# A graph layer in split fp32 matmuls: the first eight pieces of adj in two contiguous halves, with x, residual and statistics steps moved

## What is computed

```python
def _layernorm(x, axis=-1, eps=1e-05):
    m = jnp.mean(x, axis=axis, keepdims=True)
    v = jnp.var(x, axis=axis, keepdims=True)
    return (x - m) / jnp.sqrt(v + eps)

h = jnp.maximum(_layernorm(x, axis=-1), 0.0)           # x: (8192, 128) fp32
x = x + ((1.0 - 0.1) * (adj @ h) + 0.1 * L0_gnn_h)     # adj: (8192, 8192) fp32
```

## Time and profile before

| | |
|---|---|
| median of 3 runs | 717.7 us (717.62 to 717.85) |
| the profiled execution, its own time | 718.35 us |
| its span | 716.6 us |
| TensorE busy | 707.0 us (99%) |
| VectorE busy | 625.0 us (87%) |
| ScalarE busy | 521.3 us (73%) |
| read from HBM / written | 281.02 MB / 4.19 MB |
| mean over the span | 398 GB/s |
| granted TensorE clock | 1.00 |

### The profile page before, as it was taken

One profiled execution on the slowest core, in us unless ns is written; L12 is line 12 of the kernel. 1 busy time (PEld: TensorE's weight loads), 2 busy tenths in 40 slices (PEclk: granted clock), 3 DMA queues, 4 the chain that ended last, 5 costly groups with the idle time before them and its releaser, 6 DMA issues.

```text
span 716.6 us, 7886 instructions
## 1 busy us (share of the span) xinstructions
PE 707.0 (99%) x3076; PEld 575.3 (80%) x3076; DVE 625.0 (87%) x462; ACT 521.3 (73%) x342; POOL 27.6 (4%) x17
## 2 busy tenths in 40 slices
PE   7999999999999999999999999999999999999998
PEld 2777888888888888888888888888888888888886
DVE  3879998998999989998888888888888889888985
ACT  3878877869688796877767676676767767676773
POOL 1001102001020100200000000000000000000000
DMA  8999999999999999999999999999999999999991
GB/s 291 411 418 420 403 419 419 415 422 414 421 411 422 416 415 402 420 421 412 383 398 409 387 395 378 403 397 388 413 387 406 423 418 413 420 415 425 420 422 75
DMA packets 46117, 285.73 MB, mean 399 GB/s; under 512 B 5120, under 2 KB 5632, under 8 KB 14592
## 3 DMA queue, kind: packets, MB, share of 16 engines
q1 hardware_dynamic: 46080, 285.23, 98.2%
HBM read 281.02 MB, written 4.19 MB: 398 GB/s over the span
## 4 chain that ended last, share of the span: by engine, by line
PE 88%; DMA 4%; DVE 3%; issue 2%; ACT 1%; SPq 1%; POOL 0%; DVEq 0%; ACTq 0%
PE acc L428 16%; PE acc L429 16%; PE acc L433 16%; PE acc L417 13%; PE acc L412 13%; PE acc L406 13%; DMA raw<-wide_dram 4%; DVE a_lo L316 2%; SPq L190 1%; ACT a_hi L270 1%; POOL rstd L232 0%; ACT h_full L239 0%; DVE stats L282 0%; SPq L179 0%; DVE h_lo L308 0%
## 5 line engine op out<-in xcount | busy, mean ns | idle before, releaser
L316 DVE TENSOR_TENSOR a_lo<-raw,a_hi 128x2048 fp32r<-128x2048 f32 (+1 forms) x262 | 581.3, 2224 | 65.3 <-ACT a_hi L270 64.8
L270 ACT ACTIVATE a_hi<-raw 128x2048 fp32r<-128x2048 f32 (+1 forms) x262 | 487.7, 1865 | 175.3 <-PE acc L433 90.4
L428 PE MATMUL acc<-a_hi,h_hi 128*128 128x512 f32 x512 | 199.2, 389 | 0.0
L429 PE MATMUL acc<-a_hi,h_lo 128*128 128x512 f32 x512 | 199.2, 389 | 0.0
L406 PE MATMUL acc<-a_hi,h_hi 128*128 128x512 f32 x504 | 135.9, 390 | 3.0 <-ACT a_hi L270 3.0
L417 PE MATMUL acc<-a_lo,h_hi 128*128 128x512 f32 x504 | 135.8, 391 | 1.2 <-DVE a_lo L316 0.8
L433 PE MATMUL acc<-a_lo,h_hi 128*128 128x512 f32 x512 | 136.8, 389 | 0.0
L412 PE MATMUL acc<-a_hi,h_lo 128*128 128x512 f32 x504 | 134.8, 389 | 0.0
L406 PEld LDWEIGHTS acc<-a_hi,h_hi 128*128 128x128 f32 x504 | 94.1, 188 | 25.2 <-issue 2.9
L417 PEld LDWEIGHTS acc<-a_lo,h_hi 128*128 128x128 f32 x504 | 93.9, 188 | 23.8 <-DVE a_lo L316 4.6
L429 PEld LDWEIGHTS acc<-a_hi,h_lo 128*128 128x128 f32 x512 | 96.1, 188 | 20.0
(11 more groups left out here) (15 smaller groups left out, 26.9 us busy)
## 6 DMA issues: line engine op xcount, KB each, us to landing
raw<-tall_dram SPq DMA_DIRECT2D x128, 1024.0 KB, 8.7
raw<-wide_dram SPq DMA_DIRECT2D x118, 1024.0 KB, 9.8
raw<-wide_dram SPq DMA_DIRECT2D x16, 512.0 KB, 12.6
res_sb<-res_dram SPq DMA_DIRECT2D x16, 512.0 KB, 5.6
x_sb<-x_dram SPq DMA_DIRECT2D x15, 256.0 KB, 10.2
out_dram<-finished SPq DMA_DIRECT2D x15, 256.0 KB, 9.1
raw<-wide_dram SPq DMA_DIRECT2D x8, 256.0 KB, 6.4
out_dram<-finished SPq DMA_DIRECT2D x2, 128.0 KB, 1.8
```

Of the source, the lines that this page charges most:

```text
L270: nc.scalar.activation(a_hi[:, q % SPLIT_SLOTS, cols], raw[:, q % RAW_SLOTS, cols], ACT.Copy).then_inc(hi_ready, 1)
L316: nc.vector.tensor_tensor(a_lo[:, q % SPLIT_SLOTS, cols], raw[:, q % RAW_SLOTS, cols], a_hi[:, q % SPLIT_SLOTS, cols].bitcast(fp32), ALU.s ...
L428: nc.tensor.matmul(bank, h_hi[:, k, :], a_hi[:, slot, cols], start=(k == 0), stop=False)
L429: nc.tensor.matmul(bank, h_lo[:, k, :], a_hi[:, slot, cols], start=False, stop=False)
```

## The change

- Pieces 0 to 7 come in two parts of 128 x 1024 each, and the host lays each part out as one block (`early_dram`); so far pieces 0 and 1 came in four parts and 2 to 9 in two, cut out of the whole piece's layout. Pieces 8 and 9 now come whole.
- x unit 1 (blocks 4 to 7) is loaded before piece 4 instead of before piece 2; unit 2 before piece 6 instead of before piece 4.
- Statistics and aggregation of blocks 4 to 7 stand behind `a_lo` of piece 3 instead of before `h_lo` of unit 0; their shift behind piece 4, the scaling behind pieces 5 and 6, `h_lo` behind piece 7. For blocks 8 to 11 statistics start at piece 7 (was 5), the shift stands at 12 (was 10), scaling at 13 and 14 (was 12 and 13), `h_lo` at 15 (was 14).
- Residual load n stands behind piece 44 + 10n (was 12 + 12n), sum n behind 51 + 10n (was 20 + 12n), for n < 8.
- The warm-up is 15 matmuls of 256 columns (was 12 of 512).

```diff
-PARTS = {0: 4, 1: 4}
-PARTS.update({_q: 2 for _q in range(2, 10)})
+EARLY = 8
+PARTS = {_q: 2 for _q in range(EARLY)}
+PART = PIECE // 2
...
-    _d = 5 if _g == 3 else 2 * _a - 12 if _single else 2 * _a - 19
+    _d = 7 if _g == 3 else 2 * _a - 12 if _single else 2 * _a - 19
...
-        _s = _end + 3 + 2 * (_u - _a // UNIT)
+        _s = _end + (2 if _g == 3 else 3) + 2 * (_u - _a // UNIT)
...
-    RES_LOAD_AT[12 + 12 * _n if _n < RES_RING else _at - 5] = _n
-    RES_SUM_AT[20 + 12 * _n if _n < RES_RING else _at - 2] = _n
-WARM_UP = 12
+    RES_LOAD_AT[44 + 10 * _n if _n < RES_RING else _at - 5] = _n
+    RES_SUM_AT[51 + 10 * _n if _n < RES_RING else _at - 2] = _n
+WARM_UP = 15
...
-        warm = sb("warm", [P, SEG], bf16)
+        warm = sb("warm", [P, SEG // 2], bf16)
...
+                    if q in PARTS:
+                        source = adj_early[q, i, :, :]
+                    elif q < WIDE_PIECES:
+                        source = adj_wide[q - EARLY, :, :]
+                    else:
+                        source = adj_tall[q - WIDE_PIECES, :, :]
...
             load_piece(0)
             load_x(1, 1, UNIT)
-            load_piece(1)
-            load_x(2, UNIT, 2 * UNIT)
-            for q in range(NATIVE, PIECES):
+            for q in range(1, PIECES):
+                if q == 4:
+                    load_x(2, UNIT, 2 * UNIT)
...
-                if q == 4:
+                if q == 5:
                     scale_unit(1, 0)
-                if q == 5:
+                if q == 6:
                     scale_unit(1, 1)
...
-            dve.wait_ge(x_landed[2], 16)
-            for k in range(UNIT, 2 * UNIT):
-                last = statistics(k)
-            last.then_inc(stats_ready, 1)
-            aggregate(2)
             low_h(0)
             for q in range(NATIVE, PIECES):
                 low_a(q)
-                if q == NATIVE:
+                if q == 3:
+                    dve.wait_ge(x_landed[2], 16)
+                    for k in range(UNIT, 2 * UNIT):
+                        last = statistics(k)
+                    last.then_inc(stats_ready, 1)
+                    aggregate(2)
+                if q == 4:
                     make_shift(2)
-                if q == 6:
+                if q == 7:
                     low_h(1)
...
-                nc.tensor.matmul(acc[:, WIDE - 1, :], warm[:, 0:P], warm[:, :], start=True, stop=True)
+                nc.tensor.matmul(acc[:, WIDE - 1, 0:SEG // 2], warm[:, 0:P], warm[:, :], start=True, stop=True)
...
+    adj_early = np.ascontiguousarray(adj_wide[:EARLY].reshape(EARLY, P, 2, PART).transpose(0, 2, 1, 3))
```

More of the change, by code:

```diff
@@ L99, in pieces_of_chunk, with build @@
     return WIDE_PIECES + (c - WIDE + 1) * TALL_PIECES
-def build(nc, x, adj_wide, adj_tall, res, out):
+def build(nc, x, adj_early, adj_wide, adj_tall, res, out):
     fp32, fp32r, bf16 = mybir.dt.float32, mybir.dt.float32r, mybir.dt.bfloat16
@@ L186, in load_piece @@
                 for i, cols in parts(q):
-                    source = (adj_wide[q // QUADS, q % QUADS, :, cols] if q < WIDE_PIECES else
-                              adj_tall[(q - WIDE_PIECES) // TALL_PIECES, (q - WIDE_PIECES) % TALL_PIECES, :, cols])
+                    if q in PARTS:
[4 more added lines that the diff above has]
+                        source = adj_tall[q - WIDE_PIECES, :, :]
                     landed = part_landed[part_number(q, i)] if q in PARTS else raw_landed[q % RAW_SLOTS]
@@ L445 @@
         adj[:wide].reshape(QUADS, QUAD, SEG, BLOCKS, P).transpose(3, 0, 4, 1, 2)
-    ).reshape(BLOCKS, QUADS, P, PIECE)
+    ).reshape(WIDE_PIECES, P, PIECE)
+    adj_early = np.ascontiguousarray(adj_wide[:EARLY].reshape(EARLY, P, 2, PART).transpose(0, 2, 1, 3))
     adj_tall = np.ascontiguousarray(
         adj[wide:].reshape(CHUNKS - WIDE, SEG, TALL_PIECES, QUAD, P).transpose(0, 2, 4, 3, 1)
-    ).reshape(CHUNKS - WIDE, TALL_PIECES, P, PIECE)
+    ).reshape(PIECES - WIDE_PIECES, P, PIECE)
     x_t = x.reshape(CHUNKS, SEG, F).transpose(0, 2, 1)
@@ L453 @@
         "x_dram": np.ascontiguousarray(x.reshape(BLOCKS, P, F).transpose(1, 0, 2)),
-        "wide_dram": adj_wide,
+        "early_dram": adj_early,
+        "wide_dram": np.ascontiguousarray(adj_wide[EARLY:]),
         "tall_dram": adj_tall,
```

## The result

Before 717.65 us (717.33 to 717.85, 6 runs); with the change 720.48 us (718.17 to 721.12, 6 runs). The medians lie 2.8 us apart; the ratio over all runs is 1.0033 (1.0023 to 1.0043), **slower by 2.4 us**, where 715.3 was forecast and 717.6 was the upper end. The runs of the change lie 3.0 us apart, those of the kernel before 0.5.

What follows compares the result with a forecast made beforehand. The prediction took TensorE's pace of 2.72 us a piece from 79.60 us on as the bound, so gains come before it. Terms of -0.8, -0.6, -1.0 and 0 sum to -2.4 us: 715.3 us forecast, range 713.0 to 717.6.

Steps and rivals of the forecast that it cites:

- What bounds the kernel: Whole run: TensorE's pace of 2.72 us a piece from 79.60 us on; gains show in piece 23 or 24's start.
- Term 1: Behind piece 12: residual load 0 leaves, later pieces land 1.25 us earlier, of which 0.8 us comes through.
- term 2: Behind piece 20: residual sum 0 leaves VectorE's queue, which had no idle time there; -0.6 us.
- Term 3: Start: pieces 0 and 1 in contiguous halves instead of quarters make later landings earlier; -1.0 us (0 to -3.1).
- Rival C: Start: quarters cause all 3.1 us of DMA's early loss; gain 4.5 us, 713.2 us; chance 0.18.
- Parts costed at nothing: Start: later x units 1 and 2, moved statistics of blocks 4 to 7, new warm-up; no net effect expected.
- Term 4: Residual loads 1 to 7, pieces 54 to 114: SP's longer waits cost 0, covered by 0.9 us seven times.
- Rival A: Pieces 55, 65 to 115: residual waits break TensorE's pace, 1.2 us seven times, 8.4 us, giving 723.7; chance 0.13.
- the limit that I worked out: Residual waits: the fourth piece after k may land until +8.4 us from TensorE's start of k without delaying TensorE.
- Rival D: Start: a pause after the warm-up keeps TensorE's clock low, about 1 us paid, 716.3 us; chance 0.05.

Runs made afterwards that it cites:

- Experiment 6: Kernel before, with residual loads behind pieces 44 + 10n and sums behind 47 + 10n, so SP does not wait: 716.29 us, ratio 0.9975.
- experiment 2: Changed kernel with residual sum n behind piece 47 + 10n instead of 51 + 10n: 714.36 us, ratio 0.9949 to the kernel before.
- experiment 8: Against experiment 2: early halves cut out of the whole piece's layout, pieces 0 and 1 in quarters again: 716.20 us, ratio 0.9975 to the kernel before.
- experiment 9: Against experiment 2: x units 1 and 2, statistics, shifts, scalings and h_lo of blocks 4 to 11 back where they stood: 714.68 us.
- experiment 10: Against experiment 2: the old warm-up of 12 matmuls of 512 columns: 714.49 us, ratio 0.995 to the kernel before.
- experiment 4: Changed kernel with residual loads behind 44 + 12n and sums behind 53 + 12n, the wait still three pieces: 720.17 us, ratio 1.0031 to the kernel before.
- experiment 3: Kernel before with only the change's residual loads (44 + 10n) and sums (51 + 10n): 722.61 us, ratio 1.0072.

## Why the prediction was wrong, step by step

**What bounds the kernel**: right. The gain showed in when piece 23 starts, and the loss in where the pace of 2.72 us broke afterwards; the change alters nothing else.

**Term 1 (residual 0 leaves its place, -0.8) and term 2 (its sum leaves VectorE, -0.6)**: right. In the changed kernel the lead of ScalarE's pieces grows by 1.2 us between pieces 12 and 13; VectorE's `a_lo` of piece 16, forecast for 56.8, stood at

```profile
54.89 2.29 DVE L321 TENSOR_TENSOR a_lo<-raw,a_hi 128x2048 fp32r<-128x2048 f32 x1
```

3.7 us ahead of 58.57, of which 2.7 had been there at piece 12: 1.0 came through. Experiment 6 has both terms at 1.7 us for 1.4.

**Term 3 (pieces 0 and 1 in contiguous halves, -1.0)**: right in kind, too small. By landings it is 2.7 us in the change's profile, of which up to 0.4 is chance (the old start begins piece 10 between 37.16 and 37.54), by times 1.9 (experiments 2 and 8: 716.20 - 714.36 = 1.8; 2 and 6: 1.9). What was mis-sized is the part that I called unavoidable: from 2 to 5 us DMA moved 325 GB/s instead of 153. Rival C's ground ("engines that finish their part of a quarter early stand until the next is issued") was tested by no run; what is shown is that almost half of the effect is the layout, which no term of mine priced apart.

**Parts costed at nothing**: x order, statistics and warm-up, right (experiments 9 and 10).

**Term 4 (residual waits: 0, covered by 0.9 us seven times)** is the step that failed, and with it the sign: it costs 6.1 us (720.48 against 714.36), 6.3 in the kernel before. Rival A, at 0.13, has the place right, but not the condition: it wanted the first load behind a wait to take over 7.4 us to land, and the seven took 5.6 to 7.0. That its price of 8.4 came near is luck: it was 1.2 us seven times, and in the profile four waits cost 0.7, 2.3, 0.7 and 0.2. Term 4's cover of 0.9 us was worked out from one row of before and then used for all seven waits. Three things in its walk were wrong.

*How long DMA's queue lasts.* I took it from the rows of before: a load lands up to 9.7 us after its issue, so 9.4 us between two loads would hardly leave DMA idle. In the changed kernel no residual has been in the way up to piece 44, and DMA has caught up. SP's timeline ahead of the first wait, and the landings of the two loads at its top:

```profile
140.01 2.72 SPq L195 DMA_DIRECT2D raw<-wide_dram  x2
...
151.35 0.33 SPq L200 DMA_DIRECT2D res_sb<-res_dram  x1
...
151.72 0.43 SPq L195 DMA_DIRECT2D raw<-wide_dram  x1
```

```profile
DMA to landing us min/median/max: 8.2/8.2/8.2
```

The second of them, piece 54, was issued at 142.4 and had landed at 150.6; the next transfer came at 151.35. DMA slackens even before that landing and starts late behind the issue: in half microseconds from 148 us on it moves 229, 197, 98 and 98 GB/s, then none from 150 to 152, and 205 again only from 152.5. Hence the 78 GB/s. So the landing of the last piece is no safe measure of how long the queue has work: at the second and third wait the next issue came before that landing (179.8 against 182.3 us, 208.2 against 209.4), and DMA still lost 1.1 and 1.5 us.

*Every wait from the same state.* At the first one the walk holds, with more room than I gave it: piece 55 is issued at 151.72, lands 6.0 us later (forecast 6.5), and TensorE loses nothing. But I had the number that forbids treating the second and third alike, and used it in rival A only: 27.05 us of DMA work in every 27.2. What is not made up is carried on. ScalarE's waits for landings are none before 151 us, 3.0 us from 151 to 180, 8.8 us from 180 to 208. A late ScalarE makes a late VectorE, a late residual sum and so a later release of SP. The third wait, from the timeline, TensorE starting piece 71 in the first line:

```profile
205.86 1.07 PE L412 MATMUL acc<-a_hi,h_hi 128*128 128x512 f32 x4
...
207.46 0.68 DVE L329 SCALAR_TENSOR_TENSOR residual<-res_sb 128x512 f32<-128x512 f32 x1
...
208.55 0.43 SPq L195 DMA_DIRECT2D raw<-wide_dram  x1
...
214.22 1.92 ACT L275 ACTIVATE a_hi<-raw 128x2048 fp32r<-128x2048 f32 x1 [1.36 <-DMA raw<-wide_dram]
...
217.47 1.90 ACT L275 ACTIVATE a_hi<-raw 128x2048 fp32r<-128x2048 f32 x1
...
221.75 1.19 PE L423 MATMUL acc<-a_lo,h_hi 128*128 128x512 f32 x4 [0.17 <-DVE a_lo L321]
```

Piece 75 is issued 2.7 us behind TensorE's start of piece 71, not 1.0, and lands, though in only 5.6 us, at +8.3: the limit that I worked out was +8.4.

*What stands between two pieces.* Behind piece 75 ScalarE scales and rounds a unit of h, 1.4 us, and reaches piece 76 at 217.47; its `a_lo` comes 0.2 us too late, and TensorE waits for the first time by more than a moment. My walk had splits only, no scaling. The fourth wait, the dearest, shows the same on VectorE:

```profile
251.70 0.17 DVE L306 SCALAR_TENSOR_TENSOR shift<-mean_var,rstd 128x8 f32<-128x8 f32 x1 [1.53 <-POOL rstd L237]
...
254.13 1.19 PE L423 MATMUL acc<-a_lo,h_hi 128*128 128x512 f32 x4 [0.89 <-DVE a_lo L321]
```

Piece 85 was issued 2.2 us behind TensorE's start of piece 81 and landed at +9.2, past the limit of +8.4. Then, behind `a_lo` of piece 86, VectorE stood 1.5 us for GpSimd's power (`rstd`) of eight blocks, before it could shift and go on to piece 87. VectorE stands five times for that in the kernel before too, 7.6 us in all from 100 to 350 us, and it costs nothing while pieces are ahead; here 1.2 of the 2.3 us are lost right behind it.

Why two more pieces' distance per round in experiment 4 did not help is only argued: it leaves some 0.4 us per wait (12 x 2.5 + 1.25 + 0.95 = 32.2 us of DMA in 32.6; the 0.6 of its expectation is too high), against dry spells of one to four.

**Rival D** (the clock): the profile of the change has the first two of piece 0's matmuls 0.98 us apart, 4.91 and 5.89, the next 0.58, and all later ones 0.43; nothing of it reaches piece 10, and the old warm-up (experiment 10) gains nothing. The rule of the Trainium skill cited for it ("TensorE: Matmul & The Clock Gate", "Why this matters for your kernels") asks for TensorE to be kept busy before the full clock is counted on. The traces agree about the level; the 1 us that rival D made of it does not show in the time, since DMA hides it.

## What to carry to other kernels

What a wait inside the queue that issues loads can cost is what the transfer engines miss while it stands, less what the pieces land ahead of their deadlines; it is not what the waiting transfer misses. So look at what the queue still moves at that place and then, not elsewhere in the trace, and follow the whole burst and several rounds where DMA has almost no time to spare. Moving the release of a single buffer one piece earlier in another engine's program was worth 6 us here, more than all of the change's intended gains together.

## What the runs showed that I had not expected

- At the start the size and layout of the transfers matter: 153 GB/s from 2 to 5 us with quarters before, 180 with them in experiment 8, 224 with strided halves, 308 and 325 with contiguous ones. In the full flow from 13 to 32 us strided and contiguous halves alike move 411 to 416 GB/s; how quarters do there no run shows.
- A cliff: a wait of two pieces (7.6 us at the longest) costs nothing, one of three (9.6 us) 6 us.
- The runs scatter once landings set TensorE's pace: 3.0 us from fastest to slowest with the change, 4.4 in experiment 3, but only 1.2 in experiment 4; 0.4 in experiment 2.
- TensorE's level of clock came later in one profile than in the others. In experiment 8, TensorE's weight loads for piece 0 stand 0.85 us apart (two per matmul instruction of the program), the 1.2 GHz level, with the granted clock at 1.00, where the change has 0.43:

```profile
7.05 0.34 PEld L402 LDWEIGHTS acc<-raw,h_full 128*128 128x128 f32 x1 [0.52 <-issue]
7.90 0.34 PEld L402 LDWEIGHTS acc<-raw,h_full 128*128 128x128 f32 x1 [0.52 <-issue]
```

TensorE had done the same short warm-up and then stood from 4.5 to 5.2 us. So the low clock of rival D does occur. It lasted to 9.6 us and next to nothing of it reached the landings: DMA's share was 1.03 from 9 us on. In the profile of experiment 3 the clock fell later, after TensorE had stood for 1.8 us up to 14.98: the granted clock was 0.50 from 17 to 19 us, and piece 3 started at 19.96, 1.3 us later than in experiment 6; at piece 10 0.1 us of that was left.
